# The last state space layer of a twelve-layer network: decay sums from split running sums in bfloat16, and half of the score multiplications moved to GpSimd

## The reference, cut to what matters

```python
xBCzA = jnp.einsum('bld,ed->ble', input_, in_proj_w)
# xBC: causal convolution over 4 tokens, bias, silu -> x, Bm, Cm
dt = jax.nn.softplus(A_log)                 # per token and head
A_cum = jnp.cumsum(-dt, axis=-1)            # over the tokens of the chunk
Lm = jnp.exp(segsum(A))                     # exp(sum of -dt over z < k <= s), 0 above the diagonal
Y_diag = jnp.einsum('bcshn,bczhn,bhcsz,bczhp->bcshp', Cm, Bm, Lm, X)
yf = y_ssm + D * x / dt
out = jnp.einsum('bld,ed->ble', yf * silu(z + z_bias), out_proj_w)
```

## Time and profile before

| | before |
|---|---|
| median of 3 runs | 1522.03 us |
| the profiled execution, whole | 1525.09 us |
| its span | 1523.3 us |
| granted TensorE clock, mean | 0.948 of full |
| TensorE busy | 1372.9 us, 90% |
| VectorE busy | 919.2 us, 60% |
| ScalarE busy | 767.3 us, 50% |
| GpSimd busy | 528.1 us, 35% |
| the changed layer in the span | 1209 to 1428 us |
| its two unit loops, first output pair to last projection | 1274.8 to 1322.5 and 1372.1 to 1427.4 us |

### The profile page before, as it was taken

How to read it: one execution, slowest core, us unless ns; L and a number is a source line. 1 busy time by engine, 2 the same in 40 slices (tenths; PEclk the granted TensorE clock), 3 DMA queues, 4 the chain that set the end, 5 groups by cost and what they waited for, 6 DMA issues and landing times.

```text
span 1523.3 us, 24834 instructions
## 1 busy us (share of the span) xinstructions
PE 1372.9 (90%) x9246; PEld 855.1 (56%) x9264; DVE 919.2 (60%) x1713; ACT 767.3 (50%) x1847; POOL 528.1 (35%) x528
## 2 busy tenths in 40 slices
PE   7869999999888879999999998998996789988799
PEld 3434555565455545666667774664663545545536
DVE  7784322224588755545555788855787587686631
ACT  3452111111788567776776456457776455363230
POOL 3230000000277468886882000110843435414200
PEclk9979999999999999999999999998998798988899
DMA  8020211001200300000000100020001100000100
GB/s 257 26 86 1 68 53 41 1 0 60 107 2 2 126 0 8 8 8 8 8 8 1 77 23 1 1 83 2 2 2 72 56 1 2 3 0 3 30 0 28
DMA packets 21851, 48.06 MB, mean 32 GB/s; under 512 B 1506, under 2 KB 16995, under 8 KB 20580
## 3 DMA queue, kind: packets, MB, share of 16 engines
q1 hardware_dynamic: 21732, 46.47, 8.9%
HBM read 41.22 MB, written 5.24 MB: 31 GB/s over the span
## 4 chain that ended last, share of the span: by engine, by line
PE 64%; DVE 21%; ACT 6%; issue 5%; POOL 4%; DMA 0%; DVEq 0%; ACTq 0%; POOLq 0%
PE PS L890 47%; PE PS L1128 5%; DVE work L2638 4%; PE PS L1187 3%; PE PS L891 3%; ACT work L1733 2%; PE PS L987 2%; PE PS L1225 2%; DVE small L2076 2%; DVE small L2425 1%; PE PS L904 1%; DVE work L2222 1%; DVE X L2617 1%; DVE work L2606 1%; POOL work L823 1%
## 5 line engine op out<-in xcount | busy, mean ns | idle before, releaser
L890 PE MATMUL PS<-XT,WB 128*128 128x512 f32 (+1 forms) x688 | 300.8, 595 | 5.2 <-DVE XT L2102 2.9
L890 PEld LDWEIGHTS PS<-XT,WB 128*128 128x128 f32 (+1 forms) x688 | 127.1, 191 | 149.8 <-issue 146.1
L1733 ACT ACTIVATE work<-PS,small 128x128 f32<-128x128 f32 x512 | 137.7, 416 | 43.6 <-DVE small L2425 43.6
L2297 DVE TENSOR_TENSOR work<-PS,work 128x512 f32<-128x512 f32 x48 | 33.1, 691 | 170.1 <-PE PS L890 170.1
L1659 ACT ACTIVATE work<-PS 128x512 f32<-128x512 f32 x48 | 28.7, 597 | 194.6 <-PE PS L890 194.6
L2425 DVE TENSOR_REDUCE small<-PS 128x4 f32<-128x512 f32 x128 | 80.5, 684 | 36.1 <-PE PS L890 34.6
L890 PE MATMUL PS<-XT,WA 128*128 128x512 f32 (+2 forms) x224 | 97.9, 600 | 4.4 <-DVE XT L2102 2.3
L666 POOL TENSOR_SCALAR small<-small 128x4 f32<-128x4 f32 x22 | 5.1, 230 | 268.3 <-DVE small L2079 268.2
L2638 DVE SCALAR_TENSOR_TENSOR work<-PS,vec,work 128x508 f32<-128x508 f32 (+2 forms) x108 | 80.2, 743 | 13.7 <-DVE work L2638 6.5
L1128 PE MATMUL PS<-WB,work 128*128 128x256 f32 x384 | 86.9, 379 | 0.5 <-DVE work L2302 0.5
L890 PE MATMUL PS<-WA,XT 128*128 128x256 f32 (+1 forms) x384 | 81.5, 374 | 3.6 <-DVE XT L2410 1.8
(11 more groups left out here) (388 smaller groups left out, 2988.3 us busy)
## 6 DMA issues: line engine op xcount, KB each, us to landing
WB<-in_l0f SPq DMA_DIRECT2D x8, 768.0 KB, 8.1
WB<-in_l1x SPq DMA_DIRECT2D x1, 6144.0 KB, 18.3
WB<-in_l0f SPq DMA_DIRECT2D x32, 96.0 KB, 7.2
WB<-in_l2f SPq DMA_DIRECT2D x1, 3072.0 KB, 10.0
WA<-in_l3a SPq DMA_DIRECT2D x1, 2624.0 KB, 9.3
WB<-in_l3f SPq DMA_DIRECT2D x1, 2064.0 KB, 7.9
WA<-in_l1f SPq DMA_DIRECT2D x1, 2056.0 KB, 11.2
C<-in_ctx SPq DMA_DIRECT2D x2, 1024.0 KB, 7.1
```

The lines of the kernel that those rows point to most:

```text
L890: mm = lambda o, l, r, s, e: nc.tensor.matmul(o, l, r, start=s, stop=e)
L1733: f(wk(12288 + (u % 8) * G + h * P, P), bank(j)[:, h * P:(h + 1) * P], ACT.Exp, bias=sm(704 + (u % 8) * 4 + h, 1)).then_inc(*act_step(*([j ...
L2297: v.tensor_tensor(l0f_h(m)[:, lo:lo + G], bank(j), l0f_s(m)[:, lo:lo + G], ALU.mult).then_inc(*dve_step(j))
```

## The change

The decay sum of a unit becomes one bfloat16 matmul of 94 rows, 128 columns, 512 moving columns. The running sums of -dt are made once for the whole layer, for both 64-token halves (jobs "cum", two banks, 16 small products between convolutions 10 and 11 of the first half). They are split into three bfloat16 parts by ScalarE (`split_sums`: six evacuations of 64 x 512 with scale -1), TensorE subtracting each part in PSUM before the next is taken (`without_part`). SyncE parks the parts in DRAM (6 DMAs) and loads them into the operands of four units at a time (96 DMAs, two slots, each refilled when the last unit that used it is summed). The constant rows of the operands are the identity against -1e30 for later tokens (two VectorE writes, `later_tokens`), and head and half patterns (GpSimd copies). Even units' exponentials go to SBUF (`l3a_g`) instead of PSUM, their bank is freed by ScalarE, and GpSimd multiplies them there by the masked C-B products, in place; odd units stay as they were. GpSimd's step products and its copy of exchanged halves are gone.

```diff
 l += [("c", cc, g) for cc in range(11)] + ([("cum", 0), ("cum", 1)] if g == 0 else []) + \
     [("c", cc, g) for cc in range(11, 12)] + [("z", 4 * g + i) for i in range(4)] + [("ea", g)] + ...
@@ SyncE
+            sp.wait_ge(cum_parts, 6)
+            for g in range(2):
+                for part in range(3):
+                    sp.dma_start(cum_park[part, 4 * g:4 * g + 4]..., cum_part(part)[:, 4 * g:4 * g + 4]).then_inc(cum_parked[g], 16)
+            for n in range(16):
+                b, h0, into = n // 2, 32 * (n % 2), decay_in[n % 2]
+                if n % 8 == 0:
+                    sp.wait_ge(cum_parked[n // 8], 48)
+                if n < 2:
+                    sp.wait_ge(decay_rows, n + 3)
+                    sp.wait_ge(masked_rows, n + 1)
+                else:
+                    sp.wait_ge(*full(J("l3a", "seg", (n - 2) // 8, (n - 2) % 8 * 4 + 3)))
+                for part in range(3):
+                    sp.dma_start(decay_left(4 * (n % 2), 4)[64 + 8 * part:72 + 8 * part, :]..., cum_park[part, b, h0:h0 + 32]...).then_inc(into, 16)
+                    sp.dma_start(decay_right(4 * (n % 2), 4)[88 + 2 * part:90 + 2 * part, :]..., cum_park[part, b, h0:h0 + 32]...).then_inc(into, 16)
@@ GpSimd, in the second state space layer and at the start of this one
-            nc.gpsimd.tensor_copy(tri_halves[...], cst("tri", ...))                       # two
-                nc.gpsimd.tensor_copy(dt_exchanged[lo:lo + 64, :], wk(14336, 512, ...))   # two
+            nc.gpsimd.tensor_copy(r3(decay_left(0, 8)[0:64, :], 64), cst("ident", ...)...)
+            nc.gpsimd.tensor_scalar(decay_left(0, 8)[64:96, :]..., by_half..., -1.0, None, ALU.mult)
+            for slot in (0, 4):
+                nc.gpsimd.tensor_copy(decay_right(slot, 4)[64:96, :]..., by_head...)
@@ GpSimd, unit loop
-                    nc.gpsimd.tensor_tensor(r3(l3a_step(n), 64), steps.unsqueeze(2)..., tri_halves.unsqueeze(1)..., ALU.mult)
+                for u in range(0, 32, 2):
+                    if u % 8 == 0:
+                        pool.wait_ge(even_masks, 4 * g + u // 8 + 1)
+                    pool.wait_ge(*freed(job_of["l3a", "seg", g, u]))
+                    shared = l3a_cbm(0)[:, (u % 8 // 2) * 64:(u % 8 // 2 + 1) * 64]
+                    nc.gpsimd.tensor_tensor(r3(l3a_g(u), 64), r3(l3a_g(u), 64), shared.unsqueeze(1)..., ALU.mult).then_inc(even_scores, 1)
@@ TensorE
+            def running_sums():
+                pe.wait_ge(steps_ready, 1)
+                sums = [begin("l3a", "cum", half) for half in range(2)]
+                for half, o in enumerate(sums):
+                    lo = 64 * half
+                    for b in range(NB):
+                        ins = nc.tensor.matmul(o[0:64, b * 64:b * 64 + 64], wk(14336 + b * 64, 64, lo, lo + 64), cst("tri", lo, lo + 64)[:, lo:lo + 64], ...)
+                    ins.then_inc(cum_sums, 1)
+            def without_part(sums, part):
+                for half, o in enumerate(sums):
+                    pe.wait_ge(cum_parts, 2 * part + half + 1)
+                    ins = more(r3(o[0:64, :], 64), identb[0:64, 0:64], cum_part(part)[:, :, half, :], True)
+                    ...
+                    if (g, cc) == (0, 10):        # behind convolution cc
+                        running = running_sums()
+                    if (g, cc) in ((0, 0), (0, 3)):   # behind z product cc
+                        without_part(running, cc // 3)
-                            for lo in (0, 64):
-                                ins = mm(o[at:at + 64, :], cst("strict", ...)[:, lo:lo + 64], l3a_step(32 * g + u)[lo:lo + 64, :], True, True)
+                            if u % 4 == 0:
+                                pe.wait_ge(decay_in[n % 2], 96 * (n // 2 + 1))
+                            end(mm(o, decay_left(u % 8)[0:94, :], decay_right(u % 8)[0:94, :], True, True))
-                        for u in range(4 * q, 4 * q + 4):
+                        pe.wait_ge(even_scores, 16 * g + 2 * q + 2)
+                        for u in (4 * q + 1, 4 * q + 3):
                             pe.wait_ge(*freed(J("l3a", "seg", g, u)))
@@ ScalarE
+            def split_sums(part):
+                for half in range(2):
+                    ...
+                    f(cum_part(part)[:, :, half, :], r3(bank(j, 64), 64), ACT.Copy, scale=-1.0).then_inc(cum_parts, 1)
+                    if part == 2:
+                        act.wait_ge(cum_parts, 5 + half)
+                        act.sem_inc(bank_free[bank_of[j]], 1)
+                    if g == 0 and cc == 10:       # behind own tap 10 and Silu 9
+                        split_sums(0)
+                    if g == 0 and cc in (0, 3):   # behind the Silu of z cc
+                        split_sums(1 + cc // 3)
-                    f(bank(j), bank(j), ACT.Exp).then_inc(*act_step(act_to_dve))
+                    if u % 2:
+                        f(bank(j), bank(j), ACT.Exp).then_inc(*act_step(act_to_dve))
+                        continue
+                    if u >= 8:
+                        act.wait_ge(*full(J("l3a", "ya", g, (u - 8) // 4)))
+                        act.wait_ge(*full(J("l3a", "yb", g, (u - 8) // 4)))
+                    ...
+                    f(l3a_g(u), bank(j), ACT.Exp).then_inc(*act_step(j))
@@ VectorE
+                v.tensor_reduce(by_head, ...)     # and by_half, once, in an early layer
+            later_tokens(0)                       # before the dt copy
+            later_tokens(4)                       # behind it
+                            if par == 0 and t:
+                                dve.wait_ge(even_scores, 16 * g + t)
                         if t % 4 == 0:
                             dve.wait_ge(*dve_last())
-                        scores(2 * t)
+                            dve.sem_inc(even_masks, 1)
```

More of the change, by code:

```diff
@@ L133, in plans @@
     for g in range(2):
[L134 removed]
+        l += [("c", cc, g) for cc in range(11)] + ([("cum", 0), ("cum", 1)] if g == 0 else []) + \
+            [("c", cc, g) for cc in range(11, 12)] + [("z", 4 * g + i) for i in range(4)] + [("ea", g)] + \
             [("eb", g, 0), ("eb", g, 1)] + [("x", 4 * g + i) for i in range(4)]
@@ L265, in build @@
         identb, causalb, onesb = sb("identb", P, BF16), sb("causalb", 4 * P, BF16), sb("onesb", P, BF16)
-        small = sb("small", 848)
+        small, pattern = sb("small", 848), sb("pattern", 16)
         WORK = 18432
@@ L452, in l0x_decay, with decay_left, decay_right, cum_part @@
             return wk(14336 + c * G, G)
-        tri_halves, dt_exchanged = WB[:, 11424:11488], WB[:, 11488:12000]
+        def decay_left(slot, n=1):
+            return WB[0:96, 11424 + slot * 64:11424 + (slot + n) * 64].bitcast(BF16)
+        def decay_right(slot, n=1):
+            lo = slot % 4 * D
+            return (XN[0:96, lo:lo + n * D] if slot < 4 else wk(15360 + lo, n * D, 0, 96)).bitcast(BF16)
+        def cum_part(part):
+            return wkb(12288 + part * G, N, 0, 64).rearrange("p (b f z) -> p b f z", f=2, z=64)
+        by_head, by_half = pattern[64:96, 0:8], pattern[64:96, 8:10]
         def l3a_g(u):
@@ L848, in _ @@
             roots()
-            pool.wait_ge(halves_ready, 2)
-            pool.wait_ge(steps_ready, 1)
[L851 to L855, removed]
+            pool.wait_ge(*full(job_of["l3a", "ln", 1, 1]))
+            for slot in (0, 4):
+                nc.gpsimd.tensor_copy(decay_right(slot, 4)[64:96, :].rearrange("p (u h z) -> p u h z", h=8, z=64),
+                                      by_head.unsqueeze(1).unsqueeze(3).to_broadcast([32, 4, 8, 64])).then_inc(decay_rows, 1)
+                pool.wait_ge(decay_rows, 3 + slot // 4)
+            pool.wait_ge(steps_ready, 1)
             for i in range(4):
@@ L1403, in _ @@
             end(ins)
+            def running_sums():
[4 more added lines that the diff above has]
+                    for b in range(NB):
+                        ins = nc.tensor.matmul(o[0:64, b * 64:b * 64 + 64], wk(14336 + b * 64, 64, lo, lo + 64), cst("tri", lo, lo + 64)[:, lo:lo + 64],
+                                               start=b == 0, stop=True, skip_group_check=True)
+                    ins.then_inc(cum_sums, 1)
+                return sums
+            def without_part(sums, part):
+                for half, o in enumerate(sums):
+                    pe.wait_ge(cum_parts, 2 * part + half + 1)
+                    ins = more(r3(o[0:64, :], 64), identb[0:64, 0:64], cum_part(part)[:, :, half, :], True)
+                    if part:
+                        end(ins, "l3a", "cum", half)
+                    else:
+                        ins.then_inc(cum_sums, 1)
             for g in range(2):
@@ L2033, in _ @@
                     act.wait_ge(*full(j))
-                    f(bank(j), bank(j), ACT.Exp).then_inc(*act_step(act_to_dve))
+                    if u % 2:
[4 more added lines that the diff above has]
+                        act.wait_ge(*full(J("l3a", "yb", g, (u - 8) // 4)))
```

(7 more changed lines are left out.)

54 lines of the change are left out of this document (33 added, 21 removed).

## The result

| | before | changed |
|---|---|---|
| median of the runs, us | 1522.78 (4 runs, 1521.43 to 1523.72) | 1529.57 (4 runs, 1526.46 to 1531.24) |
| ratio to before | 1 | 1.0048 (95%: 1.0026 to 1.0070) |
| span of the profiled execution, us | 1523.3 | 1528.5 |
| granted TensorE clock, mean of the span | 0.948 | 0.937 |

A forecast was written before the change was run, and what follows sets the result against it. TensorE was taken to bound the unit loop, with one VectorE wait. First half +6.3, second half -8.75, together -2.4, and 1 us for issue gave -3.4: 1518.6 from 1522.03 us, own range 1515 to 1521.

The forecast's parts named there:

- first half, to the end of x: Convolutions to x's transposes: the running sums' splits start the state decay at 1262.0, not 1252.32; 9.2 us lost.
- to the first pair: First half, behind the masks: two GpSimd products cost 2.1 us, the first output pair comes 0.4 us sooner after x.
- first half's loop: First half's unit loop: shorter decay sums gain 5.5 us net, entering at 1.2 GHz loses 3.0.
- second half, to its first pair: Second half, masks' end to first output pair: pair at 1371.3 instead of 1372.05, 0.75 us gained.
- second half's loop, first pair to last projection: Second half's unit loop: shorter sums gain 5.5 us, low-clock stretches shrink for 2.5 more; 45 to 48 us, not 55.4.
- the rest, "issue" among it: Chain part called issue, 5% of the span: TensorE's stream loses 192 matmuls, 1 us gained (0 to 2).
- 3.0 lost: First half's loop entry at 1.2 GHz: first pair and C-B 2.05 and 3.0 us, next sums and lead-in 1.1 more.
- the second: Rival: the clock stays down in both loops, +15 us, 1537; 1524 where it decides; chance 0.17.
- the DMAs: Parking parts and loading operands: first loads land at 1272.7, 2 us of cover; loop refills unwaited; no loss.
- the early work: VectorE's mask tiles and GpSimd's pattern copies, placed in those engines' idle time; no loss.
- ScalarE's exponentials: Unit loop: writing 512 columns to SBUF also takes 0.6 us, waiting for the pair eight units before; no loss.
- GpSimd's multiplication: Exponentials by scores, 128 x 512: 1.04 us each, inside the loop's pace; matters only for a half's first pair.

The follow-up runs named there:

- Experiments 6: Kernel before with half of the layer's decay sums cut to 16 of 512 columns, those units' exponentials of zero: 1525.01 us, ratio 1.0018.
- 7: Residual add put ahead of the masks in four kernels: before 1515.18 us, before with fewer sums 1511.61, changed 1513.61, changed with running sums early 1504.83.
- 8: Changed kernel with the decay sums of two units ahead of each residual-add wait issued five times instead of once: 1521.48 us, ratio 1.0002.
- The early place: Changed kernel with running sums behind convolution 6 instead of 10, splits and subtractions moved earlier too: 1519.01 us, ratio 0.9992.
- the sums alone: Kernel before with only the running sums and their splits added at the changed kernel's places, parts unused: 1536.72 us, ratio 1.0083.
- experiment 9: Changed kernel with running sums early and residual add ahead of the masks, every decay sum issued twice: 1514.24 us, ratio 0.9926.
- experiment 2: Changed kernel with decay sums issued three times where TensorE waits anyway: 1526.79 us, ratio 1.0029.

## Why the prediction was wrong

By its own steps, in the two profiled executions (all differences are after minus before, and they sum to the spans' +5.2):

| step | forecast | measured |
|---|---|---|
| first half, to the end of x | +9.2 | +9.2 |
| to the first pair | -0.4 | -0.7 |
| first half's loop | -5.5 + 3.0 = -2.5 | +2.7 |
| second half, to its first pair | -0.75 | -1.1 |
| second half's loop, first pair to last projection | -5.5 - 2.5 = -8.0 | -7.1 (55.3 to 48.2) |
| the rest, "issue" among it | -1 | +2.2 |

*The step that failed* is the first half's loop: "I expect the first half to enter its loop at 1.2 GHz ... **3.0 lost**". I let the lower clock go with the first pair, the C-B products and the next sums. It stayed through the second pair too, and it came back twice in the loop (1304.4 and 1318.0 us), 24.2 us in all instead of 3.8. The rows price it. From the first pair to the sums at 1293.69 are 10.40 us, where the same work at the full clock takes 6.1: 4.3 lost, not 3.0. The pair and sums from 1304.36 to 1308.00 and the sums to the projection from 1321.07 to 1328.97 lose 1.3 and 2.9 more, which the sum had at nothing. That is 8.5; the kernel before lost 1.5 in the same way (1295.12 to 1299.90), so the term of 3.0 measured 7.0.

The row was in the table: TensorE's wait of 1.67 us for the residual add stood in the loop with 1.95 us of sums ahead of it, and both later falls come right behind that wait. I priced that wait by its length (I had it grow to 2.1, and it was 2.19), and never asked what a longer idle time beside shorter sums does to the clock. Of my rivals the second (1524 to 1537) is nearest, to which I had given 0.17, but its sign was a clock of 0.5 through whole groups of eight, and that was seen only at the entry. (Its sum for such a group starts at 14.5 us, not 15.) Experiments 6, 7 and 8 show that the low time goes with the wait and the short sums; what they left open is why the fall came in this place in one execution and elsewhere in the next.

*The loop at the full clock.* The sums' start to the next work is 0.97 us where it was 1.88, 0.91 less and not 1.05: I had taken 0.226 us from products elsewhere, and here it is 0.243. And the residual add came 0.39 us earlier, not 0.65. Six groups give 5.5, two waits longer by 0.52 take 1.0: 4.4, not 5.5. With +0.2 of "issue" the 20.4 us more at the lower clock must have cost 2.7 + 4.4 - 0.2 = 6.9, as the rows above have it, that is 0.34 us for each. The runs themselves give a like price: over 35 runs of the kernel before, the span falls by 9.2 us for each 0.01 of mean clock, which is 30 us of low time, or 0.3 for each. The smaller sets of runs of that kernel (11 and twice 17) give 0.17 to 0.36, and that the clock sets the span there is read from their going together, not tested.

*The place of the sums.* The size was right, the working not. The state decay began at 1264.04, 2.0 us later than I said, since TensorE had stood 5.11 us and z1 to z3 then ran mostly at the lower clock, 8.10 us. But decay and transposes together took 8.14 us (1264.04 to 1272.18) and not 10.73, being partly at the full clock. Two errors of 2.0 and 2.6 us cancelled, with a slip of 0.5 in my addition: 1262.0 + 7.06 + 3.67 is 1272.7, not 1272.2, so by its own terms the loss was 9.7. The early place (-10.6) and the sums alone (+8.6 on this stretch) show that the cost is of the place; how it splits into its parts I had not understood.

*Right*: the DMAs (the first decay rows were there when TensorE came, no refill was waited for), the early work, ScalarE's exponentials. GpSimd's multiplication was mis-sized, 1.24 us and not 1.04 (a mean of 1.27 over all 32):
```profile
1280.74 4.96 POOL L904 TENSOR_TENSOR work<-work 128x512 f32<-128x512 f32 x4 [44.08 <-DVEq L2938]
```
The first pair waits 0.61 us for it.

*The rest, +2.2.* In the next layer the clock was down between 1434.1 and 1440.9 us; a group of four products there takes 1.17 us in place of 0.66. That is the 2.2 us: from the last projection to the next work of L1564 are 12.6 us, where the kernel before (L1504) has 10.4. Where such a stretch falls differs from run to run: before with the add moved has the long form of this stretch too, and no run shows that the change put it there.
```profile
1437.26 1.17 PE L924 MATMUL PS<-CT,XT 128*128 128x128 f32 x4
...
1441.23 0.66 PE L924 MATMUL PS<-CT,XT 128*128 128x128 f32 x4
```

## What to carry to other kernels

When an edit makes TensorE's work shorter in a loop that has a wait in it, price the wait again: it grows by what the work ahead of it shrinks, and the idle time, now larger beside the work, can bring the clock down for stretches that cost about 0.3 us for each us here. Remove or move such a wait first (here one line that put the residual add ahead of the masks, worth 9 to 13 us of the layer in four kernels, where the waiting itself is 6.7 to 9.8), and only then shorten the work. Compare the stretch that the edit touches as well as the whole time: up to 9 us of difference between two executions lay ahead of it. And work that an edit adds to a serial stretch belongs where its engine already idles: 10 us here lay between one place and another a few jobs earlier.

## What was not expected of the hardware

- Filling a wait of 2.19 us with work that nobody needs took 17.6 us of low time out of the two loops and cost nothing (experiment 8; 2.6 us less in the loops, 8.1 by the medians). Repeated sums in a loop without that wait cost 6 to 9 us (experiment 9). Filling only 0.9 us of each wait did not lower the low time (43 us, experiment 2).
- Leaving out half of the decay sums of the kernel before gained nothing that its runs show (ratio 1.0018), with 18 us more at 1.2 GHz.
- TensorE stops for up to 2.3 us, often in the midst of like matmuls, with no semaphore that the trace names; in the layer this was 7.5 us before, 4.1 in the changed kernel and 13.9 in the one with the sums alone. What these stops wait for no run here shows.
```profile
1317.51 1.63 PE L925 MATMUL PS<-work,WB 64*32 64x64 f32 x111
1320.66 0.48 PE L925 MATMUL PS<-work,WB 64*32 64x64 f32 x17 [1.51 <-issue]
```
